# Gate scores as extra columns of the shared low-rank tile, and the first expert's w1 splits spread between the gelus of half 1

## The reference, cut to what matters

```python
xt = einsum('bct,bcd->bdt', x, cond_w[conditions]).reshape(1024, 256)
logits = xt @ gate_w                       # 8 experts
top_p, top_i = top_k(softmax(logits), 2)
for k in range(2):                         # choose, number the places, keep pos < 160
    h = gelu(buf @ w1 + b1)                # 8 experts, 256 -> 1024
    y = h @ w2 + b2 + gelu(buf @ wd) @ wu  # low-rank side path, rank 32
    out += y[e, pos] * keep * w
sh = gelu(xt @ sw1 + sb1) @ sw2 + sb2 + gelu(xt @ swd) @ swu
out = x + out + 0.2 * sh
```

## Time and profile before

| | |
|---|---|
| median of 3 runs | 193.1 us (193.08 to 193.26) |
| the profiled execution, its own time | 193.34 us |
| its span | 191.6 us |
| PE busy | 182.3 us (95%) |
| DVE busy | 137.3 us (72%) |
| ACT busy | 137.5 us (72%) |
| POOL busy | 106.9 us (56%) |
| mean granted TensorE clock | 0.992 |

### The profile page before, as it was taken

One profiled execution on the slowest core, in us unless ns is written; L12 is line 12 of the kernel. 1 busy time (PEld: TensorE's weight loads), 2 busy tenths in 40 slices (PEclk: granted clock), 3 DMA queues, 4 the chain that ended last, 5 costly groups with the idle time before them and its releaser, 6 DMA issues.

```text
span 191.6 us, 3982 instructions
## 1 busy us (share of the span) xinstructions
PE 182.3 (95%) x1410; PEld 174.5 (91%) x1410; DVE 137.3 (72%) x297; ACT 137.5 (72%) x291; POOL 106.9 (56%) x118
## 2 busy tenths in 40 slices
PE   6999999999999999999999999999999999999950
PEld 6996788998889999999999999999999999999850
DVE  4389489796455276695795896897897896879710
ACT  2256899306959306996996997998997989899400
POOL 5400005899817470140688688688788770747380
PEclk9999999999999999999999999999999999999996
DMA  4593500069903222827668767978968949851442
GB/s 145 147 331 99 205 19 0 0 227 311 317 14 96 72 68 38 294 68 248 209 74 259 225 120 226 253 127 232 248 126 246 293 56 274 233 58 14 56 43 33
DMA packets 23816, 29.23 MB, mean 153 GB/s; under 512 B 4442, under 2 KB 20564, under 8 KB 23796
## 3 DMA queue, kind: packets, MB, share of 16 engines
q1 hardware_dynamic: 19412, 23.03, 38.2%
q0 software_dynamic: 4016, 5.38, 17.5%
q10 hardware_dynamic: 368, 0.56, 1.0%
HBM read 23.92 MB, written 5.05 MB: 151 GB/s over the span
## 4 chain that ended last, share of the span: by engine, by line
PE 70%; DMA 9%; POOL 5%; DVE 4%; ACT 4%; issue 3%; SPq 2%; POOLq 1%; DVEq 0%
PE hid_ps L909 10%; PE hid_ps L911 10%; PE hid_ps L910 10%; PE y_ps L911 10%; PE y_ps L910 10%; PE y_ps L909 10%; POOL out_rows L408 5%; DMA out_rows<-y_row,slot_tok 4%; DMA gate_raw<-in_L_ffn_gate_w 3%; DMA wu_raw<-in_L_ffn_b 2%; PE turn_ps L1077 2%; ACT gelu_f L558 2%; ACT hid_h L559 1%; DVE w_l L622 1%; PE hid_ps L930 1%
## 5 line engine op out<-in xcount | busy, mean ns | idle before, releaser
L651 DVE TENSOR_TENSOR hid_l<-gelu_f,hid_h 128x320 fp32r<-128x320 f32 (+1 forms) x80 | 41.8, 534 | 19.0 <-ACT hid_h L559 18.5
L408 POOL DMA_INDIRECT out_rows<-y_row,slot_tok x24 | 41.5, 1730 | 13.4 <-DVE y_row L830 6.6
L394 POOL DMA_INDIRECT slot_in<-slot_rows,slot_src x24 | 31.7, 1320 | 21.2 <-PE turn_ps L1077 10.0
L909 PE MATMUL hid_ps<-xs_h,w_h 128*128 128x256 f32 (+2 forms) x128 | 37.9, 296 | 0.0
L558 ACT ACTIVATE gelu_f<-hid_ps,bias_s 128x320 f32<-128x320 f32 x64 | 34.8, 544 | 2.6 <-PE hid_ps L911 1.1
L910 PE MATMUL hid_ps<-xs_l,w_h 128*128 128x256 f32 (+2 forms) x128 | 36.6, 286 | 0.0
L911 PE MATMUL hid_ps<-xs_h,w_l 128*128 128x256 f32 (+2 forms) x128 | 36.6, 286 | 0.0
L909 PE MATMUL y_ps<-w_h,hid_h 128*128 128x256 f32 x128 | 36.3, 284 | 0.0
L910 PE MATMUL y_ps<-w_l,hid_h 128*128 128x256 f32 x128 | 36.2, 283 | 0.0
L911 PE MATMUL y_ps<-w_h,hid_l 128*128 128x256 f32 x128 | 36.2, 283 | 0.0
L559 ACT ACTIVATE hid_h<-hid_ps,bias_s 128x320 fp32r<-128x320 f32 x64 | 35.0, 547 | 0.0
(11 more groups left out here) (209 smaller groups left out, 375.2 us busy)
## 6 DMA issues: line engine op xcount, KB each, us to landing
w_raw<-in_L_ffn_w SPq DMA_DIRECT2D x16, 1024.0 KB
x_in<-in_x SPq DMA_DIRECT2D x2, 512.0 KB, 4.7
w_raw<-in_L_ffn_sw SPq DMA_DIRECT2D x1, 1024.0 KB
slot_rows<-token_row SPq DMA_DIRECT2D x2, 512.0 KB, 4.0
out_rows<-base SPq DMA_DIRECT2D x2, 512.0 KB
wu_raw<-in_L_ffn_wu SPq DMA_DIRECT2D x24, 32.0 KB
w_raw<-in_L_ffn_sw ACTq DMA_DIRECT2D x1, 512.0 KB
w_raw<-in_L_ffn_sw SPq DMA_DIRECT2D x1, 512.0 KB, 5.2
```

The lines of the kernel that those rows point to most:

```text
L394: pool.indirect_dma_start(out=slot_in[par][0:n, s, :], out_offset=None, in_=x_rows, in_offset=bass.IndirectOffsetOnAxis(ap=slot_src[0:n, e ...
L408: pool.indirect_dma_start(out=out, out_offset=bass.IndirectOffsetOnAxis(ap=slot_tok[0:n, e, s:s + 1].bitcast(U32), axis=0), in_=y_row[0:n, ...
L651: dve.tensor_tensor(hid_l[:, j - 1, 0:n], gelu_f[:, j % 3, 0:n], hid_h[:, j - 1, 0:n].bitcast(F32), ALU.subtract).then_inc(hid_split, 1)
L909: pe.matmul(out_ap, l_h, r_h, start=start, stop=False)
```

## The change

The gate's 16 columns are put beside the 96 of the shared low-rank tile (`LOW_GATE` is 112). Both lie, for the shared expert, in the first columns of `xs_h` and `xs_l`, which are free then. The gate's high and low part stand together in the high weights; their place in the low weights is set to zero. The scores come out on partitions 96 to 111 of the low-rank tile's bank. `score` and `gate2` are gone; `hidden(0, 0)` and `hidden(1, 0)` take the places of score(0) and score(1), so the low-rank tile of half 1 is made early too. It stays in the bank `turn_ps[1]`, and the ring of half 0 has five banks left. The turning of the scores now stands ahead of make_rows(2). In half 1 ACT and DVE no longer split the first expert's w1 ahead of the gelus but one chunk after every second hidden tile.

```diff
+        low_gate_h, low_gate_l = [x[:, :, 0:LOW_GATE] for x in (xs_h, xs_l)]
+        def wd_pair(v, par):
+            if v > 0:
+                return wd_h[par][:, :, :, :], wd_l[par][:, :, :, :]
+            return [w[:, :, 0:LOW].rearrange("p k (g r) -> p k g r", g=3) for w in (low_gate_h, low_gate_l)]
+        def made_count(u, j):
+            if u == 1 and j == 0:
+                return 2
+            return hid_count(u, j) + (1 if u == 0 and j > 0 else 0)
         def hid_ring(u):
-            return hid_ps + [row_ps, y_ps[1], turn_ps[1]] if u == 0 else hid_ps
+            return hid_ps + [row_ps, y_ps[1]] if u == 0 else hid_ps
         def hid_bank(u, j):
-            return hid_ring(u)[j % len(hid_ring(u))]
+            return turn_ps[1] if u == 1 and j == 0 else hid_ring(u)[j % len(hid_ring(u))]
...
             def gelu_tile(u, j, n, bias):
-                act.wait_ge(hid_made, hid_count(u, j))
+                act.wait_ge(hid_made, made_count(u, j))
+                if u == 1 and j == 0:
+                    act.wait_ge(y_made, HTILES)
...
-            for c in range(CHUNKS):
-                w1_chunk(1, 1, c)
             for j in range(HT):
                 gelu_tile(1, j, HALF, shared_bias)
+                if j % 2 == 1:
+                    w1_chunk(1, 1, j // 2)
...
-            dve.tensor_tensor(gate2[:, :, E:2 * E], gate_raw[:, :, :], gate2[:, :, 0:E].bitcast(F32),
-                              ALU.subtract).then_inc(gate_lo, 1)
+            dve.memset(low_gate_l[:, :, LOW:LOW_GATE].bitcast(F32), 0.0)
+            dve.tensor_tensor(low_gate_h[:, :, LOW + E:LOW_GATE], gate_raw[:, :, :],
+                              low_gate_h[:, :, LOW:LOW + E].bitcast(F32), ALU.subtract).then_inc(gate_lo, 1)
...
             def copy_scores(h):
-                dve.wait_ge(scores_made, h + 1)
-                dve.tensor_copy(scores[:, h * HALF:(h + 1) * HALF], hid_ps[h][0:2 * E, :]).then_inc(scores_copied, 1)
+                dve.wait_ge(hid_made, made_count(h, 0))
+                dve.tensor_copy(scores[:, h * HALF:(h + 1) * HALF], hid_bank(h, 0)[LOW:LOW_GATE, :]).then_inc(scores_copied, 1)
...
                 if t == 1:
                     value_tokens()
-                    w1_chunk(0, 1, 1)
-                if t == 2:
-                    w1_chunk(1, 1, 1)
-            w1_chunk(2, 1, 1)
-            w1_chunk(3, 1, 1)
             for j in range(HT):
                 split_tile(1, j, HALF)
+                if j % 2 == 1:
+                    w1_chunk(j // 2, 1, 1)
...
-            score(0)
-            make_rows(0)
-            score(1)
-            make_rows(1)
-            make_rows(2)
-            gate_tokens()
-            make_rows(3)
...
+                if u < 2 and j == 0:
+                    pe.wait_ge(gate_lo, 1)
+                    pe.wait_ge(xct_lo, (u + 1) * KD)
+                elif u > 0 or j >= len(hid_ring(0)):
                     pe.wait_ge(hid_gelu, hid_count(u, j) - len(hid_ring(u)))
...
+            hidden(0, 0, 0, 0, xct_h, xct_l, half_cols[0], HALF)
+            make_rows(0)
+            hidden(1, 0, 0, 0, xct_h, xct_l, half_cols[1], HALF)
+            make_rows(1)
+            gate_tokens()
+            make_rows(2)
+            make_rows(3)
             for h in range(2):
-                for j in range(HT):
-                    if h == 0 and j < 2:
-                        pe.wait_ge(scores_copied, j + 1)
+                for j in range(1, HT):
                     if h == 0 and j == 2:
                         pe.wait_ge(rows_copied, NT // 2)
                     hidden(h, j, 0, 0, xct_h, xct_l, cols, HALF)
```

More of the change, by code:

```diff
@@ L51 @@
 LOW = 3 * RANK
+LOW_GATE = LOW + 2 * E
 def build(nc, x, itok, cond_w, gate_w, w1, b1, w2, b2, wd, wu, sw1, sb1, sw2, sb2, swd, swu, out, slot_rows, cond_rows):
@@ L118, in build @@
         gate_raw = sb("gate_raw", [P, KD, E])
-        gate2 = sb("gate2", [P, KD, 2 * E], F32R)
         bias_rows = sb("bias_rows", [P, P])
@@ L196, in build @@
         logits_made = sem("logits_made")
-        scores_made = sem("scores_made")
         scores_copied = sem("scores_copied")
@@ L377, in wd_hi_part @@
                 pool.wait_ge(wd_in, 16 * (v + 1))
-                pool.tensor_copy(wd_h[par][:, :, :, :], wd_raw[:, :, :].unsqueeze(2).to_broadcast(
+                pool.tensor_copy(wd_pair(v, par)[0], wd_raw[:, :, :].unsqueeze(2).to_broadcast(
                     [P, KD, 3, RANK])).then_inc(wd_hi, 1)
@@ L505, in _ @@
             act.wait_ge(gate_in, 16)
-            act.activation(gate2[:, :, 0:E], gate_raw[:, :, :], ACT.Copy).then_inc(gate_hi, 1)
+            act.activation(low_gate_h[:, :, LOW:LOW + E], gate_raw[:, :, :], ACT.Copy).then_inc(gate_hi, 1)
             for c in range(CHUNKS // 2):
@@ L633, in wd_part @@
                 dve.wait_ge(wd_hi, v + 1)
-                dve.tensor_tensor(wd_l[par][:, :, :, :], wd_raw[:, :, :].unsqueeze(2).to_broadcast([P, KD, 3, RANK]),
-                                  wd_h[par][:, :, :, :].bitcast(F32), ALU.subtract).then_inc(wd_lo, 1)
+                hi, lo = wd_pair(v, par)
+                dve.tensor_tensor(lo, wd_raw[:, :, :].unsqueeze(2).to_broadcast([P, KD, 3, RANK]), hi.bitcast(F32),
+                                  ALU.subtract).then_inc(wd_lo, 1)
             def wu_part(par, v):
@@ L938, in make_rows @@
                 ins.then_inc(rows_made, 1)
[L940 to L949, removed]
             def gate_tokens():
@@ L988, in hidden @@
                     pe.wait_ge(wd_lo, v + 1)
-                if u > 0 or j >= len(hid_ring(0)):
+                if u < 2 and j == 0:
+                    pe.wait_ge(gate_lo, 1)
+                    pe.wait_ge(xct_lo, (u + 1) * KD)
+                elif u > 0 or j >= len(hid_ring(0)):
                     pe.wait_ge(hid_gelu, hid_count(u, j) - len(hid_ring(u)))
-                m = 3 * RANK if j == 0 else P
+                m = P if j > 0 else LOW if u > 1 else LOW_GATE
                 dst = hid_bank(u, j)[0:m, 0:n]
                 for k in range(KD):
-                    if j == 0:
+                    if j == 0 and u < 2:
+                        l_h, l_l = low_gate_h[:, k, :], low_gate_l[:, k, :]
+                    elif j == 0:
                         l_h, l_l = (w[:, k, :, :].rearrange("p g r -> p (g r)") for w in (wd_h[par], wd_l[par]))
@@ L1106, in map_slots @@
                 ins.then_inc(map_made, 1)
+            half_cols = [slice(h * HALF, (h + 1) * HALF) for h in range(2)]
+            hidden(0, 0, 0, 0, xct_h, xct_l, half_cols[0], HALF)
[5 more added lines that the diff above has]
+            make_rows(3)
             for h in range(2):
-                cols = slice(h * HALF, (h + 1) * HALF)
-                for j in range(HT):
-                    if h == 0 and j < 2:
-                        pe.wait_ge(scores_copied, j + 1)
+                cols = half_cols[h]
+                for j in range(1, HT):
                     if h == 0 and j == 2:
```

## The result

The changed kernel takes 193.81 us (median of 13 runs, 192.99 to 194.25) against 193.13 before (13 runs, 192.90 to 193.34). The ratio is 1.0026, with a 95% interval of 1.0018 to 1.0035: slower by a quarter of a percent, where I forecast 0.8 us faster. The runs also scatter over 1.3 us, those of the kernel before over 0.4.

The account below looks back on a forecast made before the run. The prediction took TensorE (PE) to bound the kernel, busy 182.3 of 191.6 us. It summed +0.55 at the end of half 0 and -1.365 in half 1 to -0.81, so 193.1 became 192.3 us, range 191.3 to 192.9.

Parts of the forecast that it names:

- The eight matmuls: Gate score matmuls on PE: all eight go, 8 x 0.2275 = 1.82 us less.
- the 112 columns: Low-rank tile on PE: 112 stationary columns instead of 96 cost nothing, as price goes by the 512 moving columns.
- The memset: DVE clears 32 elements ahead of the gate's low part, on the path: 0.05 us, bounds 0 and 0.1.
- make_rows(3) and Exp: Half 0: make_rows(3) on PE ends at 21.98 instead of 21.04, Exp on ACT moves from 22.62 to 23.56.
- f = 7: Last hidden tile of half 0: split ends at 36.61, PE stalls 0.76 us and takes weights at 36.64, not 36.09.
- the one at the count: PE stall at the count in half 0: reached at 27.43, last weight of the expert choice at 27.53, some 0.2 us.
- half 0: End of half 0 on PE: 0.55 us later, bounds 0.3 and 0.95.
- its own f = 7: Half 1's split for this tile at 15.09, wanted by PE at 15.10: no slack, cost 0, upper bound 0.3 us.
- at_place: POOL work before map_slots: ended at 50.95, at worst 51.9, wanted from about 53.1; by the skill's rule about a microsecond earlier.
- Moved on other queues: Next w1 transfer on SP goes at about 60.3 instead of 48.05, lands by 65.7, costs nothing by itself.
- rival 4: Slower, chance 0.08: moved w1 transfer meets expert 0's slot-row gathers, PE stalls 4.0 us, 196.3 us; decides from landing at 65.8.
- side_data: Behind DVE's chunk 2 in half 1: starts at about 55.9 as before, so POOL's gathers stay where they are.

Follow-up runs that it names:

- experiment 11: Kernel before with only the first expert's w1 splits spread, second expert's w1 transfer held until expert 0's gather landed: 193.04 us, ratio 1.0000.
- experiment 3: Changed kernel with one more SyncE wait: second expert's w1 transfer goes out only when expert 0's gather has landed; 192.64 us, ratio 0.9964.
- experiment 6: Changed kernel, w1 transfer waiting for expert 0's gather and all four ACT w2 copies ahead of the last two row copies: 191.54 us, ratio 0.9916.
- experiment 4: Changed kernel with w1 splits back ahead of half 1 and the second expert's w1 transfer held until half 1's last split: 192.59 us, ratio 0.9969.
- experiment 7: Changed kernel with w1 splits back ahead of half 1, second expert's w1 transfer held until half 1's tile 7 split: 192.54 us, ratio 0.9970.
- experiment 9: Changed kernel with w1 splits back ahead of half 1, second expert's w1 transfer held only until half 1's tile 6 split: 192.53 us, ratio 0.9966.
- experiment 10: Changed kernel with side_data ahead of the w1 chunk on DVE, instead of behind it, after tile 5 of half 1: 192.63 us, ratio 0.9971.
- experiment 2: Kernel before with only the first expert's w1 splits spread between half 1's gelus, gate scores as before: 194.46 us, ratio 1.0057.
- experiment 1: Changed kernel with the first expert's four w1 splits back ahead of half 1, scores still in the low-rank tile: 192.76 us, ratio 0.9988.
- experiment 5: Changed kernel with w1 splits ahead of half 1 and ACT's w2 copies moved between row copies, one left before Exp: 192.19 us, ratio 0.9945.
- experiment 8: Changed kernel with w1 splits ahead of half 1 and all four ACT w2 copies ahead of the last two row copies: 191.52 us, ratio 0.9914.

## Why the prediction was wrong

**What held.** The eight matmuls are gone and the 112 columns cost nothing (starts still 0.23 apart). The memset, for which I took 0.05, cost nothing either: DVE's transpose of the conditions starts 0.49 us after ACT's copy of the gate, before 0.50. make_rows(3) and Exp came where I had them, f = 7 within 0.15 us. In the changed profile everything begins 0.27 us earlier: Exp at 23.27 (forecast 23.56 less 0.27 is 23.29), the last split at 36.47 (36.34). The stall there cost 0.78 (0.76 forecast), and the one at the count was 0.34 by the starts (0.2), so half 0 ended 0.70 later by the starts (36.75 and the 0.27, against 36.32 before) and not 0.55, within my bounds. Half 1 had no stall at its own f = 7, and experiment 11 puts the price of the spread itself at nothing, within 0.2 us. at_place was ready at 50.56 instead of 50.95, although it began 0.65 later: a microsecond shorter (11.5 us instead of 12.5), as the Trainium skill's rule on the shared port pair ("SBUF — State Buffer", section "Who interferes with whom") would have it once three w1 splits have left its time; this was not tried apart. With the gather cleared, all this gives 0.7 us by experiment 3 (0.5 to 0.9 by its interval); I had 0.8.

**What failed.** The step in "Moved on other queues" that let the moved w1 transfer cost "nothing by itself", and with it the argument against rival 4: "the gather is issued before the transfer". I compared the starts of two issues 0.7 us apart. The gather's own issue on POOL takes 1.0 to 1.4 us, so the transfer (60.35) came before its end (60.97), and the landing moved from about 3.2 us (experiment 6, whose gather takes as long to issue) to 6.2. The landing at 65.78 is the point that I had named for rival 4, 65.8. The price there is not the 4.0 us that I gave it, but 1.14 (experiment 3). This is the miss: -0.7 without it (experiment 3) and +1.14 for it give +0.4; the ratio says +0.5 (0.35 to 0.68).

A second error stood beside it. I wrote that side_data "starts at about 55.9, as before, so POOL's gathers stay where they are", and took this for harmless. Relative to PE, which came 0.9 us earlier, they were late: without the spread the last gather was issued at 58.7 (experiments 4, 7, 9), and there even a slowed gather (experiment 9) landed in time. The chunk of w1 ahead of side_data is only part of this: with the two exchanged (experiment 10) the first gather came 0.42 us earlier, but the first two took 1.25 us each to issue instead of 1.07 and 1.09, and the last one still started at 59.51. The loss needs the spread alone (1.1 us in experiment 2); the scores alone have no such wait (experiment 1).

**Rival 4 had 0.08.** The trace of before showed the gather's three issues, their length, and that the transfer would come within them. What it didn't show was the landing. I took 4.0 us from another kind of DMA, so the slack looked like 1.4 us at worst, and then priced the collision only as "a megabyte in front". With the landing unknown and a 1 MB transfer put within a microsecond of the gather, the rival deserved far more.

**What stays open.** Why the order at the end of the gather's issue decides. That the weights' packets get ahead of the gather's on the DMA engines fits, but it was only argued. The margins tried near the end of the issue are -0.62 (two kernels), -0.02, +0.06 and +0.13 us, one profile each. Why the gather's issue takes 1.38 us in the changed kernel and 0.99 before: it took 1.35 to 1.38 in five profiles with the spread (the changed kernel, experiments 2, 3, 6 and 11) and 0.99 in all without it, so the spread goes with it. VectorE's chunk ran beside it (58.88 to 60.17 without a pause), but in experiment 10 one did too (59.06 to 60.35) and the issue took 1.04. And why experiment 1 stands 0.2 us by the medians and 0.4 by the ratios above experiments 4, 7 and 9, which differ from it only by a later transfer; the intervals overlap.

## What to carry to other kernels

A chunk of work that is moved to a free place on its engine takes with it every transfer that waits for it. List those, put each at its new time, and see what else is then in flight: here the splits cost nothing where they were put, and the 1 MB behind them cost 1.1 us. Where an indirect gather is near, look at the end of its issue, not only at the start. And when PE gets faster, look for the latest thing on every other engine that PE will meet: a copy order that had slack before (Exp behind two weight copies) held back about 1 us of a possible 1.6, and cost nothing to change.

## What the runs showed of the hardware that was not expected

A gather of 64 rows of 1 KB (the last of three, the others have 128) landed 2.8 to 3.2 us after the start of its issue when the 1 MB transfer went out at the end of that issue or later, or 10 us ahead of it (experiments 5, 6, 7, 8 and 10), and 5.4 to 6.4 us after it when the transfer went out 0.6 to 1.2 us before the issue ended (the changed kernel, experiments 2 and 9). A difference of 0.6 us between two issues made 3 us in the landing. A matmul stall cost more than the idle time that the list of waits shows: 0.92 shown and 1.14 paid at the turning of slots, 0.52 shown and 0.78 paid at f = 7. The clock is not the reason: the granted clock was 1.00 both from 46 to 67 us, which holds the first of these, and from 21.5 to 46 us, which holds the second.
